# The global row normalised at the end, scored by halves, and more rounding on VectorE

## The chip, the cores and the metric

The kernel runs on one core of a Trainium2 chip. The metric is the device time of one execution in microseconds (us). A core has TensorE (PE) for matrix products, VectorE (DVE), ScalarE (ACT) and GpSimd (POOL) for elementwise work, and queues for DMA. Work in one engine is in program order; engines wait for each other by semaphores.

## What is computed

Two sequences of 1024 tokens (the model's batch of two) go through a two-layer transformer with banded attention, then a retention block and a mixture of experts. The change lies in the attention. Each of 12 heads (16 wide) attends to a window of 128-token blocks, and token 0 is "global": all see it, and it sees all 1024 keys, without a window. That second part is the "global row":

```
qg = q[:, :, g]                                     # g = token 0
sfull = jnp.einsum('bhgd,bhsd->bhgs', qg, k) + bias
og = jnp.einsum('bhgs,bhsd->bhgd', jax.nn.softmax(sfull, axis=-1), v)
out = out.at[:, :, g].set(og)
out = out.transpose(0, 2, 1, 3).reshape(b, s, d)
return out @ Wo.T + bo
```

For the windows, `softmax(scores)` is computed as exponentials in float32, which are split into a float16 value and a float16 rest, and both parts are multiplied with the values.

## The kernel before

The program makes four layer passes (2 sequences x 2 layers), and each runs the same code. In a pass there are a front (projections, transposes of q and k), U = 96 **units**, one for each block n of 128 queries and head h (u = 12n + h), and then the closing part (output projection y, norms, feed-forward). The last 12 units belong to block 7, whose window has two blocks (256 columns); the others have 384, or 256 for block 0.

The order is written by hand. Each engine's program calls its own `step(s)` for s from -24 to 113, and a unit passes through the engines with a fixed lag:

- **TensorE** at step s makes the scores of unit s into one of three banks (L1639 and L1642; it waits for the exponentials of unit s - 3) and then the value products of unit s - 4 (L1663; it waits for that unit's rounded parts). L1658 opens a group of six heads.
- **ScalarE** at step s takes the exponential of unit s twice: into p32 (float32, L806) and, for units that GpSimd serves, into p1 (float16, L808). A ring of six buffers (RING) holds them.
- **GpSimd** computes p2 = p32 - p1 for unit s - 1 (L609).
- **VectorE** serves each sixth unit (SHARE = 6: u % 6 == 5) in their place, at step u + 2: it casts p32 to p1 (L1127) and subtracts (L1128). It also combines each six heads (L1112, L1114, then L1152 at the end of the step).

From step ROW = 72 on, the global row goes through the same engines. TensorE multiplies the query of token 0 (q0s, one 12-column weight matrix for each head) with 1024 keys in two halves of 512: L1539, steps 72 to 83, one head a step, both halves, into banks 0 and 1. So both banks are complete only at step 83. VectorE takes the maxima (L1081 at step 84, L1131 and the minimum of the negated ones L1132 at step 85), ScalarE the exponentials with their sums (L772 at step 87, L775 at step 88), VectorE adds the sums, takes the reciprocal (L1084, L1085) and multiplies the 12 x 1024 row with it (L1086, step 89). TensorE transposes the row (L1546, step 91), ScalarE and VectorE make its float16 value (L779) and rest (L1090), and TensorE multiplies them with the values (L1554, steps 93 and 94, eight products each). VectorE selects each head's part (L1100, step 95, into og; rows 0 to 11 hold the value, 12 to 23 the rest). Last, six small products (L1567, L1569, step 100) sum the 24 rows of og with a column of ones.

Between them, at step 98, TensorE starts the output products y 0 and y 1 (L1413, L1414), which reuse banks 0 and 1 and therefore wait for L1100. After step 100 come the last transposes of att (L1622, L1623) and the sequence of y blocks, norms and feed-forward, in which VectorE adds and normalises what TensorE delivers.

## Time and profile before

| what | value |
|---|---|
| time, median of 3 runs | 891.1 us (891.08 to 892.95) |
| the profiled execution | 893.38 us, span of the core's work 891.6 us |
| TensorE products (PE) | 800.6 us, 90% of the span |
| TensorE weight loads (PEld) | 615.4 us, 69% |
| VectorE | 631.7 us, 71% |
| ScalarE | 561.2 us, 63% |
| GpSimd | 561.2 us, 63% |
| mean granted clock of TensorE | 0.964 of full |

The busy times are sums over the whole program; each stage has its own limit. The views used below are the timeline (start and duration of instructions on one engine, neighbours of one kind merged, and in brackets how long the engine was idle before and what ended that), and windows (busy time of each engine in a stretch, with the mean granted clock). The clock of TensorE has two levels, full (2.4 GHz) and half (1.2 GHz).

### The profile page before, as it was taken

Reading aid. Unit: us, or ns where it says so; the run is one execution under the profiler, and the core shown is the slowest. Engines: PE = TensorE matmul, PEld = TensorE weight load, DVE = VectorE, ACT = ScalarE, POOL = GpSimd, SP = SyncE. Lnnn points to the kernel's source line nnn. Section 1 sums busy time; section 2 is a strip of 40 time slices with the busy share of each in tenths; the row PEclk is TensorE's granted clock in tenths of the full one; section 3 lists DMA queues with packets and bytes.
Section 4 is the critical chain, followed back from the end, with each engine's and each line's share of the span. In section 5 each row is a group of like instructions: output and inputs, shape, how many; then the busy total and the mean of one; then the engine's idle time right before and its main releaser. Section 6 shows DMA issues by size and latency. Waiting matters only on the chain.

```text
span 891.6 us, 23616 instructions
## 1 busy us (share of the span) xinstructions
PE 800.6 (90%) x8467; PEld 615.4 (69%) x8467; DVE 631.7 (71%) x1903; ACT 561.2 (63%) x1558; POOL 561.2 (63%) x820
## 2 busy tenths in 40 slices
PE   6989999999999989989999889999998899786496
PEld 3767757667777666667777557777775568775495
DVE  4899956447999565568998462689993765987553
ACT  4878883348788843267888743678887444465264
POOL 5568876443488855464888663527886754767354
PEclk9999996999999979999999999999999999998699
DMA  3300020512000002330000006100000060501330
GB/s 81 104 8 4 3 52 4 167 40 80 3 4 3 22 26 98 109 94 26 4 3 3 22 1 203 52 33 4 3 4 2 1 202 1 214 2 60 93 106 25
DMA packets 38660, 43.84 MB, mean 49 GB/s; under 512 B 7227, under 2 KB 33946, under 8 KB 38410
## 3 DMA queue, kind: packets, MB, share of 16 engines
q1 hardware_dynamic: 18124, 19.30, 7.2%
q10 hardware_dynamic: 18148, 18.29, 6.6%
q0 software_dynamic: 2272, 4.74, 1.7%
q8 instruction: 69, 1.13, 0.5%
q14 instruction: 47, 0.38, 0.1%
HBM read 20.70 MB, written 21.59 MB: 47 GB/s over the span
## 4 chain that ended last, share of the span: by engine, by line
PE 64%; DVE 21%; POOL 5%; issue 4%; ACT 4%; DMA 2%; POOLq 0%; SPq 0%; DVEq 0%; ACTq 0%
PE bank L1419 7%; DVE p L1128 6%; PE bank L1590 5%; DVE nmx L1119 5%; PE bank L1663 5%; PE bank L1639 5%; PE bank L1714 4%; PE bank L1715 4%; PE bank L1528 4%; PE bank L1539 3%; PE bank L1593 3%; PE bank L1753 2%; PE bank L1642 2%; PE bank L1762 2%; DVE p L1127 2%
## 5 line engine op out<-in xcount | busy, mean ns | idle before, releaser
L609 POOL TENSOR_TENSOR p<-p 128x384 f16<-128x384 f32 (+1 forms) x320 | 286.0, 914 | 95.3 <-ACT p L808 91.4
L1119 DVE TENSOR_REDUCE nmx<-bank 128x1 f32<-128x384 f32 (+1 forms) x384 | 190.2, 510 | 14.0 <-PE bank L1593 9.4
L806 ACT ACTIVATE p<-bank 128x384 f32<-128x384 f32 (+1 forms) x384 | 170.2, 451 | 46.9 <-PE bank L1642 31.9
L1639 PE MATMUL bank<-stack 103*128 103x128 bf16 x1056 | 144.5, 221 | 5.3 <-ACT p L808 4.3
L808 ACT ACTIVATE p<-bank 128x384 f16<-128x384 f32 (+1 forms) x320 | 144.5, 452 | 0.0
L1642 PE MATMUL bank<-bandb,idb 128*128 128x128 bf16 x672 | 134.8, 221 | 0.0
L1590 PE MATMUL bank<-stack 100*128 100x384 bf16 (+1 forms) x384 | 120.3, 313 | 7.2 <-DVE nmx L1119 2.9
L1663 PE MATMUL bank<-vst,p 128*128 128x49 bf16 x2112 | 115.6, 185 | 9.5 <-DVE p L1128 9.1
L1663 PEld LDWEIGHTS bank<-vst,p 128*128 128x128 f16 x2112 | 89.4, 97 | 26.9 <-DVE p L1128 15.0
L1639 PEld LDWEIGHTS bank<-stack 103*128 103x128 bf16 x1056 | 87.8, 98 | 28.0 <-issue 15.6
L1593 PE MATMUL bank<-bandb,idb 128*128 128x128 bf16 x672 | 100.5, 219 | 0.0
L559 POOL TENSOR_TENSOR rstd<-ve,colc 128x1 f32<-128x1 f32 x64 | 35.1, 549 | 94.7 <-DVE ve L962 94.7
L1593 PEld LDWEIGHTS bank<-bandb,idb 128*128 128x128 bf16 x672 | 65.5, 97 | 20.5
L820 ACT ACTIVATE stack<-bank 96x1024 bf16<-96x1024 bf16 x64 | 65.1, 1017 | 19.3 <-PE bank L1528 17.8
L873 ACT ACTIVATE hid<-bank 128x512 f32<-128x512 f32 x48 | 28.7, 597 | 75.1 <-PE bank L1715 75.1
L1204 DVE TENSOR_TENSOR bank<-bank,resid 128x192 f32<-128x192 f32 x64 | 23.1, 360 | 71.4 <-PE bank L1419 71.4
L1528 PE MATMUL bank<-idb,hid 128*96 128x128 bf16 x768 | 59.1, 221 | 10.8 <-POOL hid L626 5.9
L1419 PE MATMUL bank<-w2s,hid 128*128 128x192 f32 x384 | 65.9, 328 | 3.0 <-ACT hid L873 1.7
L1528 PEld LDWEIGHTS bank<-idb,hid 128*96 128x96 bf16 x768 | 50.8, 123 | 24.2 <-issue 17.6
L1419 PEld LDWEIGHTS bank<-w2s,hid 128*128 128x128 f32 x384 | 62.2, 190 | 6.9 <-issue 5.1
L1642 PEld LDWEIGHTS bank<-bandb,idb 128*128 128x128 bf16 x672 | 65.3, 97 | 0.8
L1128 DVE TENSOR_TENSOR p<-p 128x384 f16<-128x384 f32 (+1 forms) x64 | 63.4, 991 | 2.2
(248 smaller groups left out, 1801.2 us busy)
## 6 DMA issues: line engine op xcount, KB each, us to landing
xs<-zrow ACTq DMA_DIRECT2D x8, 2193.0 KB, 12.6
xt<-xs SPq DMA_DIRECT2D x23, 129.0 KB
w2s<-in_w SPq DMA_DIRECT2D x4, 576.0 KB
mwbs<-in_mwb SPq DMA_DIRECT2D x1, 2064.0 KB, 8.7
mw2s<-in_mw SPq DMA_DIRECT2D x1, 2048.0 KB, 13.0
lnrow<-in_lnr SPq DMA_DIRECT2D x4, 480.0 KB
stack<-mtr SPq DMA_DIRECT2D x96, 3.0 KB
w1b<-in_w SPq DMA_DIRECT2D x4, 291.0 KB
```

The costliest lines, as they stand in the source:

```text
L609: nc.gpsimd.tensor_tensor(p2[:, u % RING, 0:w], p32[:, u % RING, 0:w], p1[:, u % RING, 0:w], ALU.subtract).then_inc(p2_pool, 1)
L806: ins = nc.scalar.activation(p32[:, s % RING, 0:w], ps[2 + s % 3][:, 0:w], ACT.Exp)
L808: ins = nc.scalar.activation(p1[:, s % RING, 0:w], ps[2 + s % 3][:, 0:w], ACT.Exp)
L1119: nc.vector.tensor_reduce(nmx[:, vn % 3, h:h + 1], nat_bank(v)[:, 0:w], AX.X, ALU.max, negate=True).then_inc(max_done, 1)
L1128: nc.vector.tensor_tensor(p2[:, u % RING, 0:w], p32[:, u % RING, 0:w], p1[:, u % RING, 0:w], ALU.subtract).then_inc(p2_dve, 1)
L1419: ins = mm(y, hid[:, m, blk(n % BPC)], w2s[:, m, :], start=m == 0, stop=m == FF // P - 1)
L1528: ins = nc.tensor.transpose(psb[3 + (3 * b + g) % 2][0:NPIECE, blk(h)], nat[:, b % 2, g * HG + h, :], idb[:, :])
L1590: mm(s_ps[:, 0:len(win) * P], q, stack[0:K_NAT, H + h, blk(win[0], len(win))], start=True, stop=False)
L1593: ins = mm(s_ps[:, blk(i)], idb[:, :], bandb[:, 0 if m < n else 1, :], start=False, stop=(i, m) == edges[-1])
L1639: ins = mm(ps[2 + s % 3][:, blk(i)], stack[0:K_ALL, H + h, blk(m)], stack[0:K_ALL, h, blk(n)], start=True, stop=m == n)
L1642: ins = mm(ps[2 + s % 3][:, blk(i)], idb[:, :], bandb[:, 1 if m < n else 0, :], start=False, stop=True)
L1663: ins = mm(out_ps, pt[:, w % RING, blk(a)], vst[:, m, h, :], start=False, stop=i == HH - 1 and a == len(win) - 1 and pt is p2)
```

## The change

Three things, in each of the four layer passes:

1. **Scores by halves.** The 24 products of the global row are made in another order: in steps 72 to 77 all twelve heads against the first half of the keys (bank 0), in steps 78 to 83 against the second half (bank 1), two a step as before. The semaphore f_mm counts twice. q0s holds each query twice (weights of 24 columns), so that the row's scores, maxima and exponentials stand in 24 rows, and the sum is there in all 24. VectorE writes q0s with two instructions.
2. **No scaling of the row.** L1086 is gone. The steps of the chain move: the maximum of bank 0 to step 80, that of bank 1 and the minimum to step 84, the exponentials from 87 and 88 to 85 and 86, the transposes from 91 to 89 (they wait for the exponentials alone), the float16 parts and the products with the values two steps up as well. The reciprocal is taken at step 92, and the six small products at step 100 use it in place of the ones.
3. **More units on VectorE.** Of the last twelve units, each third (86, 89, 92, 95) instead of each sixth (89, 95) is rounded by VectorE. ScalarE and GpSimd leave out their part of units 86 and 92.

```diff
+EXTRA = 3
+def on_dve(u):
+    return u % SHARE == SHARE - 1 or u >= U - 2 * SHARE and u % EXTRA == EXTRA - 1
...
@@ ScalarE
-                        if s == ROW + 15:
+                        if s == ROW + 13:
                             act.wait_ge(f_max, at(f_max, 1))
-                            nc.scalar.activation(pfull[:, 0, 0:CH], ps[0][0:H, :], ACT.Exp, bias=fst[:, 0:1],
+                            nc.scalar.activation(pfull[:, 0, 0:CH], ps[0][0:2 * H, :], ACT.Exp, bias=fst[:, 0:1],
                                                  accum_out=fst[:, 1:2]).then_inc(f_exp, 1)
...
-                            if s % SHARE != SHARE - 1:
+                            if not on_dve(s):
                                 ins = nc.scalar.activation(p1[:, s % RING, 0:w], ps[2 + s % 3][:, 0:w], ACT.Exp)
...
@@ VectorE
+                        for i in range(2):
+                            ins = nc.vector.tensor_scalar(
+                                q0s[0:K_NAT, :, :].rearrange("p a b -> p (a b)")[:, i * H:2 * H * H:2 * H + 1],
+                                stack[0:K_NAT, 0:H, 0], colc[0:K_NAT, 1:2], colc[0:K_NAT, 2:3], ALU.mult, ALU.add)
+                        ins.then_inc(glob_ready, 1)
...
+                        if s == ROW + 8:
+
+                            dve.wait_ge(f_mm, at(f_mm, 1))
+                            nc.vector.tensor_reduce(fst[:, 2:3], ps[0][0:2 * H, :], AX.X, ALU.max, negate=True)
                         if s == ROW + 12:
...
+                            dve.wait_ge(f_mm, at(f_mm, 2))
+                            ch.link(nc.vector.tensor_reduce(fst[:, 3:4], ps[1][0:2 * H, :], AX.X, ALU.max, negate=True))
+                            nc.vector.tensor_tensor(fst[:, 0:1], fst[:, 2:3], fst[:, 3:4], ALU.min).then_inc(f_max, 1)
...
+                        if s == ROW + 20:
+                            dve.wait_ge(f_exp, at(f_exp, 2))
+                            ch.link(nc.vector.tensor_tensor(fst[:, 3:4], fst[:, 1:2], fst[:, 2:3], ALU.add))
+                            nc.vector.reciprocal(fst[:, 0:1], fst[:, 3:4]).then_inc(f_norm, 1)
...
@@ TensorE
-                            for c in range(NC):
-                                ins = mm(ps[c][0:H, :], q0s[0:K_NAT, h, :], stack[0:K_NAT, H + h, c * CH:(c + 1) * CH],
-                                         start=h == 0, stop=h == H - 1)
-                            if h == H - 1:
+                            c, h = divmod(NC * h, H)
+                            for k in range(h, h + NC):
+                                ins = mm(ps[c][0:2 * H, :], q0s[0:K_NAT, k, :], stack[0:K_NAT, H + k, c * CH:(c + 1) * CH],
+                                         start=k == 0, stop=k == H - 1)
+                            if h + NC == H:
                                 ins.then_inc(f_mm, 1)
-                        if s == ROW + 19:
-                            pe.wait_ge(f_norm, at(f_norm, 1))
+                        if s == ROW + 17:
+                            pe.wait_ge(f_exp, at(f_exp, 2))
                             for n in range(NB):
-                                ins = nc.tensor.transpose(ps[0][:, n * H:(n + 1) * H], pfull[:, 1, blk(n)], idf[0:H, 0:H])
+                                ins = nc.tensor.transpose(ps[0][:, n * H:(n + 1) * H], pfull[0:H, 0, blk(n)], idf[0:H, 0:H])
...
+                            pe.wait_ge(f_norm, at(f_norm, 1))
                             for i in range(3):
-                                mm(ps[2][0:DLO, 0:1], og[:, i, 0:DLO], ones[0:2 * H, 0:1], start=i == 0, stop=i == 2)
+                                mm(ps[2][0:DLO, 0:1], og[:, i, 0:DLO], fst[:, 0:1], start=i == 0, stop=i == 2)
```

On VectorE of the first layer pass, from the maximum of the global row to the row's last use there, this stood in a row before (fst holds maxima and sums, p32, p1 and p2 the exponentials and their two parts, bank7 and den belong to a combine):

```order
L1081 TENSOR_REDUCE fst<-bank0 12x1
L1127 CAST p1<-p32 128x384
L1128 TENSOR_TENSOR p2<-p32,p1 128x384
L1131 TENSOR_REDUCE fst<-bank1 12x1
L1132 TENSOR_TENSOR fst<-fst 12x1
L1112 TENSOR_REDUCE bank7<-bank7 128x96
L1114 RECIPROCAL den<-bank7 128x6
L1152 TENSOR_TENSOR att<-bank7,den 128x96
L1084 TENSOR_TENSOR fst<-fst 12x1
L1085 RECIPROCAL fst<-fst 12x1
L1086 TENSOR_SCALAR hid<-hid,fst 12x1024
```

and this now, from the maximum of bank 1 on:

```order
L1097 TENSOR_REDUCE fst<-bank1 24x1
L1098 TENSOR_TENSOR fst<-fst 24x1
L1142 CAST p1<-p32 128x384
L1143 TENSOR_TENSOR p2<-p32,p1 128x384
L1127 TENSOR_REDUCE bank7<-bank7 128x96
L1129 RECIPROCAL den<-bank7 128x6
L1142 CAST p1<-p32 128x256
L1143 TENSOR_TENSOR p2<-p32,p1 128x256
L1164 TENSOR_TENSOR att<-bank7,den 128x96
L1101 TENSOR_TENSOR f12<-bank0,f12 128x8x12
```

The maximum of bank 0 and the multiplication of hid are no longer there, and a cast and subtraction of unit 86 stand inside the combine.

A little later on VectorE, before, from the float16 rest of the row (f12) to L1100's og:

```order
L1090 TENSOR_TENSOR f12<-bank0,f12 128x8x12
L1112 TENSOR_REDUCE bank6<-bank6 128x96
L1114 RECIPROCAL den<-bank6 128x6
L1152 TENSOR_TENSOR att<-bank6,den 128x96
L1100 TENSOR_TENSOR og<-bank1,own 24x3x96
L1100 TENSOR_TENSOR og<-bank0,own 24x3x96
```

and now:

```order
L1101 TENSOR_TENSOR f12<-bank0,f12 128x8x12
L1142 CAST p1<-p32 128x256
L1143 TENSOR_TENSOR p2<-p32,p1 128x256
L1105 TENSOR_TENSOR fst<-fst 24x1
L1106 RECIPROCAL fst<-fst 24x1
L1127 TENSOR_REDUCE bank6<-bank6 128x96
L1129 RECIPROCAL den<-bank6 128x6
L1142 CAST p1<-p32 128x256
L1143 TENSOR_TENSOR p2<-p32,p1 128x256
L1164 TENSOR_TENSOR att<-bank6,den 128x96
L1115 TENSOR_TENSOR og<-bank1,own 24x3x96
L1115 TENSOR_TENSOR og<-bank0,own 24x3x96
```

The sum and reciprocal of fst have come in between, and the cast and subtraction of unit 92 stand between the combine of bank 6 and og.

On ScalarE, before, from unit 86's exponentials to the float16 value of the row (f12):

```order
L806 ACTIVATE p32<-bank4 128x256
L808 ACTIVATE p1<-bank4 128x256
L772 ACTIVATE hid,fst<-bank0,fst 12x512
L806 ACTIVATE p32<-bank2 128x256
L808 ACTIVATE p1<-bank2 128x256
L775 ACTIVATE hid,fst<-bank1,fst 12x512
L806 ACTIVATE p32<-bank3 128x256
L808 ACTIVATE p1<-bank3 128x256
L806 ACTIVATE p32<-bank4 128x256
L806 ACTIVATE p32<-bank2 128x256
L808 ACTIVATE p1<-bank2 128x256
L779 ACTIVATE f12<-bank0 128x8x12
```

and now, from unit 84's:

```order
L817 ACTIVATE p32<-bank2 128x256
L819 ACTIVATE p1<-bank2 128x256
L783 ACTIVATE hid,fst<-bank0,fst 24x512
L817 ACTIVATE p32<-bank3 128x256
L819 ACTIVATE p1<-bank3 128x256
L786 ACTIVATE hid,fst<-bank1,fst 24x512
L817 ACTIVATE p32<-bank4 128x256
L817 ACTIVATE p32<-bank2 128x256
L819 ACTIVATE p1<-bank2 128x256
L817 ACTIVATE p32<-bank3 128x256
L819 ACTIVATE p1<-bank3 128x256
L790 ACTIVATE f12<-bank0 128x8x12
```

The two exponentials of the global row (hid) have moved from behind units 86 and 87 to behind units 84 and 85, unit 86 (the first of bank4) has no p1, and the float16 value comes before unit 89 instead of behind unit 90.

## Rows read from the trace of the kernel before

**Rows 1.** Timeline, TensorE, first layer's tail: start, duration, what [idle before <-releaser].

```profile
128.09 0.60 PE L1539 MATMUL bank<-stack,q0s 100*12 100x512 bf16 x2
...
133.15 0.23 PE L1639 MATMUL bank<-stack 103*128 103x128 bf16 x1 [1.07 <-ACT p L808]
...
134.95 1.03 PE L1546 MATMUL bank<-idf,hid 12*128 12x12 f32 x8 [1.36 <-DVE hid L1086]
...
137.46 2.13 PE L1554 MATMUL bank<-vst,f 128*24 128x294 bf16 x8
...
142.76 0.57 PE L1413 MATMUL bank<-woa,ata 96*128 96x192 f32 x2
```

**Rows 2.** Windows: stretch, length, busy of PE, PEld, DVE, ACT, POOL, clock, DMA.

```profile
132.10:134.95 2.85, 0.45 (x7) 0.34 (x7) 1.48 (x7) 2.85 (x11) 1.54 (x3) 0.87 0.60 165
134.20:141.00 6.80, 6.05 (x43) 4.39 (x44) 2.67 (x7) 3.37 (x13) 3.61 (x5) 0.50 0.02 4
687.10:690.60 3.50, 3.50 (x30) 2.72 (x29) 0.94 (x2) 1.57 (x5) 2.54 (x4) 0.51 0.00 0
```

**Rows 3.** Timeline, VectorE, first layer's tail.

```profile
128.73 0.68 DVE L1081 TENSOR_REDUCE fst<-bank 12x1 f32<-12x512 f32 x1 [1.08 <-PE bank L1539]
...
130.03 0.56 DVE L1128 TENSOR_TENSOR p<-p 128x384 f16<-128x384 f32 x1
...
131.22 0.55 DVE L1132 TENSOR_TENSOR fst<-fst 12x1 f32<-12x1 f32 x1
...
134.16 0.74 DVE L1086 TENSOR_SCALAR hid<-hid,fst 12x1024 f32<-12x1024 f32 x1
134.83 0.27 DVE L1127 CAST p<-p 128x256 f16<-128x256 f32 x1
135.13 0.78 DVE L1128 TENSOR_TENSOR p<-p 128x256 f16<-128x256 f32 x1
...
140.24 0.47 DVE L1112 TENSOR_REDUCE bank<-bank 128x96 f32<-128x288 f32 x1 [3.68 <-PE bank L1663]
...
141.76 0.81 DVE L1100 TENSOR_TENSOR og<-bank,own 24x288 f32<-24x288 f32 x2 [0.68 <-PE bank L1554]
143.06 0.53 DVE L1127 CAST p<-p 128x256 f16<-128x256 f32 x1 [0.49 <-ACT p L806]
```

**Rows 4.** Timeline, ScalarE, first layer's tail: the row's exponentials.

```profile
131.80 0.68 ACT L772 ACTIVATE hid<-bank,fst 12x512 f32<-12x512 f32 x1 [0.53 <-DVE fst L1132]
...
133.00 0.66 ACT L775 ACTIVATE hid<-bank,fst 12x512 f32<-12x512 f32 x1
```

**Rows 5.** Timeline, TensorE, tails of the second and the third layer pass.

```profile
311.69 0.60 PE L1539 MATMUL bank<-stack,q0s 100*12 100x512 bf16 x2
...
326.70 0.57 PE L1413 MATMUL bank<-woa,ata 96*128 96x192 f32 x2
...
498.49 0.60 PE L1539 MATMUL bank<-stack,q0s 100*12 100x512 bf16 x2
...
509.86 1.18 PE L1554 MATMUL bank<-vst,f 128*24 128x294 bf16 x8
...
512.07 0.57 PE L1413 MATMUL bank<-woa,ata 96*128 96x192 f32 x2
```

**Rows 6.** Timeline, GpSimd, first layer's tail, unit 94.

```profile
142.78 0.67 POOL L609 TENSOR_TENSOR p<-p 128x256 f16<-128x256 f32 x1 [1.31 <-ACT p L808]
```

**Rows 7.** Instructions on the tile q0s, VectorE: xcount, duration ns min/median/max.

```profile
L1065 DVE TENSOR_SCALAR q0s<-stack,colc x4: 303/304/305, 24.7 to 576.6; 100x12 bf16<-100x12 bf16 x4
```

**Rows 8.** Windows, 7 us around two other waits of TensorE.

```profile
383.25:390.25 7.00, 5.02 (x33) 3.64 (x32) 2.87 (x8) 3.47 (x6) 5.45 (x11) 0.76 0.33 86
567.10:574.10 7.00, 5.41 (x50) 4.20 (x51) 4.49 (x13) 4.91 (x10) 3.94 (x10) 1.00 0.35 93
```

**Rows 9.** Windows, 9 us from the y blocks on, first and third layer pass.

```profile
146.00:155.00 9.00, 8.51 (x35) 7.61 (x34) 8.23 (x31) 3.66 (x11) 7.48 (x14) 0.62 0.01 3
515.30:524.30 9.00, 7.08 (x37) 5.07 (x36) 8.24 (x31) 3.67 (x11) 7.45 (x14) 1.00 0.00 0
```

56 lines of the change are left out of this document (22 added, 34 removed).

## Prediction

> **What bounds the kernel now.** I read the page's busy shares first: TensorE 90%, no other engine above 71%. Then I looked for places where TensorE stands idle, and took the timeline of the end of a layer, engine by engine. Times below are those of the first layer pass; the other three repeat it, shifted.
>
> From unit 72 to unit 83 TensorE is packed: one step of scores, value products and two L1539 products every 1.07 us, no wait. The last L1539 starts at 128.09 [rows 1]. Then TensorE waits 1.07 us for ScalarE's exponentials and, 1.6 us later, 1.36 us for VectorE's L1086 [rows 1]. Of the 2.85 us before the L1546 transposes only 0.45 are busy [rows 2]. The clock follows: TensorE ran at full clock (2.4 GHz) until then, and then at half (1.2 GHz) for 6.8 us; the shortest such stretch of the four layers is 3.5 us [rows 2]. So the L1554 products stand in a slow stretch. What releases the transposes is one chain through the global row: L1539 ends, maximum of bank 0 (L1081, 128.73), behind it unit 83's rounding, maximum of bank 1, minimum until 131.77 (L1132) [rows 3]; ScalarE's two exponentials of the row, at 131.80 and 133.00, with unit 87's pair between them [rows 4]; the sum, the reciprocal, and L1086 from 134.16 to 134.90 [rows 3]. The output products y 0 and y 1 start at 142.76 [rows 1]. I measure a tail from the last L1539 to that L1413: 14.67 us here, 15.01 in the second layer, 13.58 in the third [rows 5]; the fourth repeats the third within 0.05.
>
> **Scores by halves, maximum earlier.** The number of L1539 products stays; bank 0 is finished six steps sooner, its maximum (0.68 us) moves into VectorE's idle time before 128.73, at no cost: were that cover gone it would cost its 0.68. Bank 1's maximum starts where bank 0's did: 128.73 + 0.68 + 0.55 for the minimum + 0.05 of hand-over gives 130.0 instead of 131.77. Queued behind it on VectorE is unit 83's rounding, which ran from 129.64 and now starts at 130.0, so unit 83's value products come about 0.4 us later. The weights become 24 columns wide instead of 12; no row of before shows such a load, but loads lie beside products that last 0.60 us in pairs [rows 1], and I price it at nothing.
>
> **Exponentials at steps 85 and 86.** ScalarE then never waits for the maximum (0.53 us before). From L772 at 131.80 to L775 at 133.00 is 1.20 us with one pair between [rows 4]. From 130.05 the same 1.20 puts the second half at 131.25 and its sum at 132.0. Queued behind: unit 85's pair ends at 131.35, which holds unit 88's scores for 0.15 us. The transposes, moved up by two steps and waiting only for the exponentials, start at 132.05 instead of 134.95.
>
> **The multiplication goes.** L1086 (0.74 us [rows 3]) and the wait for it disappear; what is late next is the copy of the transposed row: it now stands on ScalarE behind the second half (131.25, 0.66 us), one activation of unit 86 (0.26, half of the 0.52 that a pair takes in the 1.20) and the pairs of units 87 and 88, so it starts at 133.2 and ends near 133.45. VectorE's subtraction ends near 133.85. In between TensorE does units 89 and 90 and waits 0.5 us in two pieces. The 16 L1554 products start at 133.9 instead of 137.46. At full clock eight of them last 1.18 us (509.86) against 2.13 at half clock [rows 1, 5]. The third layer's stretch from 509.86 to 512.07, at full clock, holds eight of them, two steps, L1658 and four units' remaining products in 2.2 us; at that pace the sixteen, five steps, L1658 and the two transposes of att take 4.2, and TensorE stands behind unit 95's scores and unit 91's products at 138.1.
>
> **Units 86 and 92 on VectorE.** ScalarE is rid of two activations, GpSimd of two subtractions; neither is what TensorE waits for there. VectorE gets two pairs. A cast took 0.27 to 0.53 us, a subtraction of this width 0.78; the nearest lower bound is 0.56, of a wider one at 130.03 in an idle stretch of GpSimd [rows 3]. Unit 86 lands in a gap of VectorE and ends with the copy above: nothing. Unit 92 does cost. It stands after the combine L1112, which waits for unit 89's products (now 137.4), and ahead of L1100. So: combine until 138.0, unit 92 until 139.05 to 139.3, the rest of the combine 0.25, L1100 0.81 [rows 3], and y 0 starts at 140.3 at the earliest. TensorE stands idle from 138.1 but for 0.25 us of units 92 and 93. Without this unit L1100 would be ready near 139.1: about 1.1 us of the gain is given away. I take y 0 at 140.5, a tail of 12.4 us; with the lower bound of the subtraction 12.0, with 0.5 more 12.9.
>
> Here the rows show engines in each other's way: the cast at 143.06 took 0.53 us, with a subtraction of GpSimd on from 142.78 [rows 3, 6], and the one at 134.83 took 0.27. The Trainium skill (SBUF — State Buffer, section "Who interferes with whom") says that the two engines take one port pair in turn and that the later one is blocked until the earlier has finished. By that rule unit 92's cast would wait for the whole 0.67 us of GpSimd's unit 93 and every tail would be 12.9 us, 2.0 us worse in the sum, 888.9; by the row, 0.26 us of delay, it is 12.4. The trace of 143.06 agrees, since that subtraction had 0.39 us left.
>
> **One instruction more at a layer's front**: q0s is written twice. The instruction lasts 0.30 us [rows 7]; between nothing and 0.30 a layer. I take 0.3 us in all, since TensorE has other work queued there.
>
> **The sum.** Tails: 14.67 - 12.4 = 2.3, then 2.6, 1.2 and 1.2: 7.3 us. Less 0.3 at the fronts: 7.0. All of it reaches the end, because the y blocks behind start in the same order and later loads were finished long before.
>
> **What the clock does decides the rest.** The idle time between 138.1 and 140.5 is 2.1 us with 0.25 busy in it, and right behind stand the one-column products L1567. Before, 2.4 us with 0.45 busy brought the clock down in all four layers [rows 2]; elsewhere some 2.0 us of standing idle were followed by a fall (mean clock 0.76) and 1.6 us were not (1.00) [rows 8]. The new 2.1 us come in two pieces and are near to both cases. So I expect a fall, but not in each layer: in two of the four. A stretch of 3.5 us at half clock costs half of it, 1.75, where TensorE is on the path; here y 2 has some 0.4 to spare before VectorE wants it, so 1.4. Two falls: 2.8. Forecast: 7.0 - 2.8 = 4.2 us. The profiled execution took 893.4 us with a span of 891.6, 2.3 above the median of 891.1; the falls need not be the same in number in each execution. I take the 4.2 from the median: 886.9.
>
> **Rivals.**
> - The clock never falls in the tails: what speaks for it is that 1.6 us of standing idle passed without a fall [rows 8], and that the new stretch is cut by two units' products. Then the 7.0 stay, and the first layer's y stretch can win too: it ran at a mean clock of 0.62 where the third's ran at 1.00, with TensorE busy for 8.5 of nine us against 7.1 [rows 9]; of these 1.4 I count 1.2. 891.1 - 8.2 = 882.9. Chance 0.22.
> - The clock falls in all four: 7.0 - 5.6 = 1.4, so 889.7. For it: 2.1 us are as long as the 2.0 us after which it fell [rows 8], and the layers are alike. Chance 0.18.
> - Slower. Unit 92, kept out by GpSimd's units 93 and 94, delays L1100 to near 141 (tail 12.9 to 13.2); the long idle brings the clock down in each layer (1.4), and it stays down through the y stretch of one layer more than before, for 1.2, the first layer's price. Then the four tails, 56.8, less 4 x 13.05 are 4.6 gained; 5.6, 1.2 and 0.3 are lost: 2.5 slower, 893.6. With three more y stretches slow it would be 4.9 slower. It decides from the point at which y 0 starts after about 140.8. Chance 0.10.
> - Nothing arrives: the tail is set by the exponentials, scores and GpSimd's subtractions alone, whatever the row does. Against it: TensorE's second wait names L1086 and no exponential. The order of instructions shows the move made. 891.1. Chance 0.05.
>
> **Numbers.** Forecast 0.45 (884.5 to 889.2), the others as given. Measurement can tell 0.2%, 1.8 us, from no change: faster is below 889.3, slower above 892.9. Faster: 0.45 + 0.22 + 0.05 of the all-fall case = 0.72; same 0.18; slower 0.10. The range for 8 in 10 holds the forecast, the no-fall case and most of the all-fall case: 882.0 to 890.5, the low end for tails of 12.0 where no clock falls.
>
> **What would show it.** Right: in each tail the waits of 1.07 and 1.36 are gone, the transposes (L1546's successor) start 3.8 to 4.1 us after the last row product, the L1554 products run at full clock and 3.5 us earlier, and a new idle stretch of 1.5 to 2.5 us stands before y 0, released by VectorE's subtraction of unit 92 and by L1100 under its new number. Wrong: the slow stretch stays around the L1554 products; the transposes wait for ScalarE past 133; y 0 starts later than 13 us after the last row product without a slow clock; or the fronts of the layers grow by more than 0.3 us.

## The result, and the profile after

| | before | after |
|---|---|---|
| time, median of 19 runs each | 893.07 us (889.39 to 898.84) | 887.14 us (883.03 to 891.76) |
| ratio, with its 95% interval | | 0.9936 (0.9918 to 0.9954) |
| the profiled execution | 893.38 us, span 891.6 | 884.74 us, span 883.0 |
| TensorE products | 800.6 us | 792.0 us |
| mean granted clock of TensorE | 0.964 | 0.976 |

The kernel became faster by 5.9 us; 4.2 were forecast. The time lies 0.2 us from the forecast of 886.9, but the forecast was taken from a median of 891.1 (3 executions), and over 19 that of the kernel before is 893.07. So the closeness is in part luck, and it says little about the reasons, as the experiments show. The two profiled executions differ by 8.6 us, more than the medians, and of the 19 executions of the changed kernel the profiled one has the highest mean granted clock: 0.976, with a median of 0.969 and a lowest of 0.964. So the breakdown below is of a pair in favour of the changed kernel, and how many slow stretches its usual execution has is not shown.

A **tail** is the stretch from the start of the last pair of row products to the start of y 0, as in the prediction. A **slow stretch** is one in which TensorE's granted clock is half. A **y block** is one of the output products with the norm behind it.

The line numbers moved. On TensorE: L1539 is now L1552 (row products), L1546 is L1559 (transposes), L1554 is L1567 (products with the values), L1639 is L1653 (scores), L1663 is L1677 (value products), L1413 is L1425 (y 0). On VectorE: L1097 and L1098 are the second maximum and the minimum, L1142 and L1143 cast and subtraction, L1164 the end of a combine, L1115 writes og. On ScalarE L783 and L786 are the row's exponentials. L620 is GpSimd's subtraction.

The first layer's tail on TensorE, to be held against [rows 1]:

```profile
128.63 0.60 PE L1552 MATMUL bank<-stack,q0s 100*24 100x512 bf16 x2
...
131.91 0.23 PE L1653 MATMUL bank<-stack 103*128 103x128 bf16 x1 [0.39 <-ACT p L819]
...
132.62 0.66 PE L1559 MATMUL bank<-idf,hid 12*128 12x12 f32 x8
...
133.40 0.26 PE L1677 MATMUL bank<-vst,p 128*128 128x49 bf16 x4
...
133.68 0.37 PE L1677 MATMUL bank<-vst,p 128*128 128x49 bf16 x4
134.31 2.13 PE L1567 MATMUL bank<-vst,f 128*24 128x294 bf16 x8 [0.27 <-DVE f L1101]
...
136.97 1.22 PE L1567 MATMUL bank<-vst,f 128*24 128x294 bf16 x8
...
140.78 0.37 PE L1677 MATMUL bank<-vst,p 128*128 128x49 bf16 x8 [0.79 <-DVE p L1143]
141.71 0.56 PE L1425 MATMUL bank<-woa,ata 96*128 96x192 f32 x2 [0.56 <-issue]
```

Counted from the last row product, the transposes start at 3.99 us (6.86 before), the products with the values at 5.68 (9.37 before), y 0 at 13.08 (14.67 before). But TensorE still waits: 0.39 and 0.27 us early, 0.79 for VectorE's subtraction of unit 92, and 0.56 before y 0. The first eight L1567 last 2.13 us as L1554 did, at half clock. The slow stretch has begun before the 0.27 us, at 133.67 (mean clock 0.83 from 133 to 134 us): the four L1677 at 133.68 already last 0.37 us where those at 133.40 last 0.26. In the third layer, to be held against [rows 5], the same places are these:

```profile
492.40 0.60 PE L1552 MATMUL bank<-stack,q0s 100*24 100x512 bf16 x2
...
498.08 1.18 PE L1567 MATMUL bank<-vst,f 128*24 128x294 bf16 x8 [0.37 <-DVE f L1101]
...
504.28 0.56 PE L1425 MATMUL bank<-woa,ata 96*128 96x192 f32 x2 [0.56 <-issue]
```

Here the eight products last 1.18 us and y 0 starts at 11.88. The windows say why (stretch, length, busy time and count of PE, PEld, DVE, ACT and POOL, mean granted clock, DMA). After:

```profile
128.63:141.71 13.08, 10.97 (x144) 7.65 (x142) 7.71 (x22) 8.35 (x30) 7.29 (x11) 0.87 0.29 74
134.00:137.00 3.00, 2.73 (x18) 1.54 (x17) 1.96 (x5) 0.85 (x4) 1.39 (x3) 0.50 0.15 42
315.00:318.00 3.00, 2.78 (x16) 1.62 (x17) 1.87 (x5) 0.85 (x4) 1.30 (x3) 0.50 0.01 3
492.40:504.28 11.88, 9.68 (x144) 7.05 (x142) 7.71 (x22) 8.35 (x30) 7.30 (x11) 1.00 0.01 2
383.00:392.00 9.00, 8.79 (x83) 6.52 (x82) 7.42 (x22) 7.58 (x15) 5.86 (x13) 1.00 0.38 113
146.00:155.00 9.00, 7.09 (x33) 4.44 (x32) 8.10 (x31) 3.52 (x9) 8.16 (x16) 1.00 0.01 2
```

Before, the same kind of stretch, from the last row product to y 0, in the first and the third layer:

```profile
128.09:142.76 14.67, 12.08 (x145) 8.48 (x142) 7.36 (x19) 9.21 (x32) 8.23 (x11) 0.77 0.26 67
498.49:512.07 13.58, 10.99 (x144) 7.67 (x142) 7.36 (x19) 9.20 (x32) 8.22 (x11) 0.87 0.01 2
```

Before, TensorE was idle for 2.59 us of each tail (14.67 - 12.08, and 13.58 - 10.99). After, it is idle for 2.11 in the first (13.08 - 10.97) and for 2.20 in the third (11.88 - 9.68). The idle time fell by 0.4 to 0.5 us, while the tails fell by 1.59, 1.86, 1.70 and 1.66 us, 6.81 in sum. What fell is for the most part the time that the products take: before, every tail has a stretch at half clock, of 6.8 us in two layers and 3.4 in two; after, the first two tails have one of 3.4 us and the last two have none.

The rest of the 8.6 us: the y blocks of the first layer run at full clock now (the 146 to 155 window, 0.62 in [rows 9]), the third layer's do not (the next fence), 0.83 less in sum over the four, from y 0 to the first feed-forward product; a slow stretch between the second and the third pass is gone (383 to 392, clock 1.00; 0.76 in [rows 8]), 1.9 us.

```profile
505.70:512.50 6.80, 6.80 (x36) 6.43 (x35) 5.33 (x20) 1.25 (x6) 3.36 (x6) 0.50 0.01 2
```

So the third pass is not without a fall: it came 1.4 us behind y 0, after the waits of 0.79 and 0.56, lasted 6.8 us, and took 11.72 us where the other passes take 10.94 from y 0 to the first feed-forward product. In the fourth pass one of 3.4 us stands there, at 690.0, and costs nothing (10.93).

The first layer's last row product stands 0.54 us later than before. The added instruction on q0s is not the reason: behind it VectorE goes on at 25.17 us against 25.15, as far apart as the two kernels were ahead of it, and from there to the 55th microsecond they stay 0.02 to 0.03 us apart. Then 0.43 us of it arise at one cast of VectorE, of the first unit that it rounds (before, then after):

```profile
55.94 0.27 DVE L1127 CAST p<-p 128x256 f16<-128x256 f32 x1
```

```profile
55.97 0.70 DVE L1142 CAST p<-p 128x256 f16<-128x256 f32 x1
```

In both kernels a subtraction of GpSimd had started 0.12 us earlier. Before, that one took 0.93 us and the cast 0.27; after, it took 0.67 and the cast 0.70, and TensorE waited 0.66 us instead of 0.23 for this unit. The instructions of the two kernels are the same here, and in ten of the twelve other kernels of this study the cast takes 0.27, in e11 and e12 0.69. So this is an accident of the execution, not an effect of the change.

### The profile page after: what moved, and what is told of

It is laid out like the page before. It is cut to its first block, busy times and chain, and to the rows that moved or that the text cites. A ratio compares the mean times of both kernels' runs of the same rounds, so it can differ in the third digit from the quotient of the medians.

```text
span 883.0 us, 23620 instructions
## 1 busy us (share of the span) xinstructions
PE 792.0 (90%) x8467; PEld 610.7 (69%) x8467; DVE 634.1 (72%) x1919; ACT 556.7 (63%) x1550; POOL 553.2 (63%) x812
## 4 chain that ended last, share of the span: by engine, by line
PE 61%; DVE 21%; issue 6%; POOL 5%; ACT 4%; DMA 2%; POOLq 0%; SPq 0%; ACTq 0%; DVEq 0%
PE bank L1431 7%; DVE p L1143 6%; PE bank L1604 5%; DVE nmx L1134 5%; PE bank L1653 4%; PE bank L1677 4%; PE bank L1728 4%; PE bank L1729 4%; PE bank L1540 4%; PE bank L1552 3%; PE bank L1607 3%; PE bank L1656 2%; PE bank L1767 2%; PE bank L1776 2%; DVE p L1142 2%
## 5 line engine op out<-in xcount | busy, mean ns | idle before, releaser
L620 POOL TENSOR_TENSOR p<-p 128x384 f16<-128x384 f32 (+1 forms) x312 | 278.1, 911 | 92.2 <-ACT p L819 83.7
L1653 PE MATMUL bank<-stack 103*128 103x128 bf16 x1056 | 142.5, 219 | 2.5 <-ACT p L819 1.6
L819 ACT ACTIVATE p<-bank 128x384 f16<-128x384 f32 (+1 forms) x312 | 141.2, 452 | 0.0
L1677 PE MATMUL bank<-vst,p 128*128 128x49 bf16 x2112 | 115.3, 185 | 12.8 <-DVE p L1143 12.5
L1677 PEld LDWEIGHTS bank<-vst,p 128*128 128x128 f16 x2112 | 88.8, 96 | 29.8 <-DVE p L1143 18.8
L1653 PEld LDWEIGHTS bank<-stack 103*128 103x128 bf16 x1056 | 87.2, 97 | 23.7 <-issue 14.6
L1143 DVE TENSOR_TENSOR p<-p 128x384 f16<-128x384 f32 (+1 forms) x72 | 67.8, 942 | 2.5
L1540 PE MATMUL bank<-idb,hid 128*96 128x128 bf16 x768 | 58.7, 219 | 10.8 <-POOL hid L637 5.9
```

Source lines behind the costliest of these rows:

```text
L620: nc.gpsimd.tensor_tensor(p2[:, u % RING, 0:w], p32[:, u % RING, 0:w], p1[:, u % RING, 0:w], ALU.subtract).then_inc(p2_pool, 1)
L819: ins = nc.scalar.activation(p1[:, s % RING, 0:w], ps[2 + s % 3][:, 0:w], ACT.Exp)
L1143: nc.vector.tensor_tensor(p2[:, u % RING, 0:w], p32[:, u % RING, 0:w], p1[:, u % RING, 0:w], ALU.subtract).then_inc(p2_dve, 1)
L1540: ins = nc.tensor.transpose(psb[3 + (3 * b + g) % 2][0:NPIECE, blk(h)], nat[:, b % 2, g * HG + h, :], idb[:, :])
L1653: ins = mm(ps[2 + s % 3][:, blk(i)], stack[0:K_ALL, H + h, blk(m)], stack[0:K_ALL, h, blk(n)], start=True, stop=m == n)
L1677: ins = mm(out_ps, pt[:, w % RING, blk(a)], vst[:, m, h, :], start=False, stop=i == HH - 1 and a == len(win) - 1 and pt is p2)
```

## The experiments

Two theories stood against each other. By the **chain theory** the gain is what the prediction summed: the row's chain is shorter, so y 0 comes earlier. By the **clock theory** the chain's length hardly matters; what was lost before was products at half clock behind a long idle stretch, and an edit that breaks up that stretch gives the same gain with the chain as it was. The tails of all kernels that ran, from the last row product to y 0 in each of the four layer passes of the profiled execution:

| kernel | tails, us | sum | ratio to before (95%) |
|---|---|---|---|
| before | 14.67 15.01 13.58 13.54 | 56.80 | 1 |
| the changed kernel | 13.08 13.15 11.88 11.88 | 49.99 | 0.9936 (0.9918 to 0.9954) |
| e1, row only | 12.94 12.93 12.94 12.94 | 51.75 | 0.9929 (0.9907 to 0.9951) |
| e2, rounding only | 14.67 14.08 14.92 14.04 | 57.71 | 1.0010 (0.9994 to 1.0026) |
| e3, row scaled | 14.31 15.28 14.57 14.62 | 58.78 | 1.0057 (1.0035 to 1.0080) |
| e4, head by head | 11.89 11.96 13.07 13.08 | 50.00 | 0.9915 (0.9894 to 0.9936) |
| e5, og first | 11.17 12.41 11.17 11.17 | 45.92 | 0.9915 (0.9889 to 0.9940) |
| e7, waits filled | 11.85 11.92 11.85 11.85 | 47.47 | 0.9926 (0.9908 to 0.9944) |
| e8, before, filled | 12.07 12.06 12.07 12.06 | 48.26 | 0.9925 (0.9907 to 0.9943) |
| e9, unit 91, og first | 12.66 12.67 11.14 12.67 | 49.14 | 0.9920 (0.9895 to 0.9946) |
| e10, og first, filled | 11.29 11.36 11.29 11.29 | 45.23 | 0.9864 (0.9845 to 0.9882) |
| e11, y filled too | 11.27 11.34 11.27 11.27 | 45.15 | 0.9868 (0.9849 to 0.9886) |
| e12, row only, filled | 12.38 12.39 12.39 12.39 | 49.55 | 0.9913 (0.9900 to 0.9926) |
| e13, row scaled, filled | 13.24 13.31 13.24 13.24 | 53.03 | 0.9955 (0.9937 to 0.9972) |

Kernels e1 to e4 shared a chip and a set of runs of the kernel before, so did e5 to e9, and so did e10 to e13. Medians of before were 891.48, 888.98 and 892.49 us in the three. Ratios are comparable across them only within their intervals. The tails are those of one profiled execution of each kernel.

### e1: the row's part alone

The changed kernel with units 86 and 92 left to ScalarE and GpSimd.

```diff
-EXTRA = 3
+EXTRA = 6
```

> The changed kernel, but units 86 and 92 are rounded by GpSimd and ScalarE as before (EXTRA = 6). My theory (the gain is the row's chain; unit 92 on VectorE gives about 1 us a layer back): the stretch from the last row product to y 0 shrinks from 11.9 us (a layer pass of the changed kernel without a slow clock in it) to 10.8 to 11.1, and the time is 3 to 4 us below the changed kernel's: ratio to before 0.989 to 0.991. Rival (the relief of ScalarE and GpSimd carries part of the gain): ScalarE's two further activations push the row's float16 copy back by 0.26 us or more, the stretch stays at 11.9 or grows, ratio 0.993 to 0.997.

885.68 us, a ratio of 0.9929 against 0.9936 with the rounding on VectorE: the rounding adds nothing to the time that can be measured. The 10.8 to 11.1 us expected did not come, since no tail ran at full clock. TensorE, first layer's tail:

```profile
134.99 1.65 PE L1567 MATMUL bank<-vst,f 128*24 128x294 bf16 x8 [0.46 <-DVE f L1101]
...
141.22 0.27 PE L1677 MATMUL bank<-vst,p 128*128 128x49 bf16 x4 [0.23 <-POOL p L620]
141.85 0.27 PE L1677 MATMUL bank<-vst,p 128*128 128x49 bf16 x4 [0.35 <-POOL p L620]
```

The waits of 0.79 and 0.56 us at the tail's end have become 0.23 and 0.35, for GpSimd. In exchange the wait before L1567 grew from 0.27 to 0.46 and every one of the four tails has a slow stretch. Against a tail of the changed kernel with a slow stretch (13.08, 13.15) these are only 0.14 to 0.21 us shorter. The window of the first:

```profile
129.03:141.97 12.94, 11.41 (x145) 7.70 (x142) 6.07 (x17) 8.75 (x32) 7.50 (x12) 0.87 0.28 74
```

TensorE is idle for 1.53 us (12.94 - 11.41), against 2.11 to 2.20 in the changed kernel. So the two units on VectorE do cost it some 0.6 us of waiting a tail, and here most of that is taken back by the slow stretch, which falls on more products. An estimate for e1's tail at full clock is that idle time plus the 9.68 us that the products take in the changed kernel's third tail: 11.2 us.

### e2: the rounding alone

The kernel before, with its row as it was, and units 86 and 92 on VectorE.

```diff
+EXTRA = 3
+def on_dve(u):
+    return u % SHARE == SHARE - 1 or u >= U - 2 * SHARE and u % EXTRA == EXTRA - 1
...
-                            if s % SHARE != SHARE - 1:
+                            if not on_dve(s):
...
-                        if 0 <= u < U and u % SHARE == SHARE - 1:
+                        if 0 <= u < U and on_dve(u):
```

> The kernel before with the third part of the change alone: VectorE rounds units 86, 89, 92, 95. My theory: nothing waits for ScalarE or GpSimd there, unit 92 stands ahead of the selection of og, so each tail grows by 0.5 to 1.1 us (third layer pass 13.6 to 14.1 or more) and the ratio to before is 1.002 to 1.005. Rival (this part brings the gain): tails shorter, ratio 0.994 to 0.998.

892.02 us, no difference, and not the 1.002 to 1.005 expected. The waits of 1.07 and 1.35 us stand as they were. So the third part of the change does nothing to the time that can be measured, alone or on top of the rest.

### e3: the multiplication put back

The changed kernel, but the row is scaled before its transposes, as before; everything else keeps its new place.

```diff
+                        if s == ROW + 15:
+                            dve.wait_ge(f_exp, at(f_exp, 2))
+                            ch.link(nc.vector.tensor_tensor(fst[:, 3:4], fst[:, 1:2], fst[:, 2:3], ALU.add))
+                            ch.link(nc.vector.reciprocal(fst[:, 3:4], fst[:, 3:4]))
+                            nc.vector.tensor_scalar(pfull[:, 1, :], pfull[:, 0, :], fst[:, 3:4], None,
+                                                    ALU.mult).then_inc(f_norm, 1)
...
-                            pe.wait_ge(f_exp, at(f_exp, 2))
+                            pe.wait_ge(f_norm, at(f_norm, 1))
```

> The changed kernel with the row scaled before the transposes again (sum, reciprocal, multiplication at step 87; the small products use the column of ones). My theory: the transposes start at 5.0 to 5.2 us after the last row product instead of 4.0, the L1567 products 0.7 to 1.0 us later, tails 0.7 to 1.0 us longer, time 3 to 4 us above the changed kernel's: ratio to before 0.996 to 0.998. Rival (the copy behind ScalarE's exponentials hides the multiplication): the L1567 products start within 0.3 us of where they did, ratio 0.993 to 0.995.

895.96 us: slower than the kernel before, and outside what either side expected. TensorE, first layer's tail:

```profile
131.81 0.23 PE L1654 MATMUL bank<-stack 103*128 103x128 bf16 x1 [0.39 <-ACT p L819]
...
133.62 0.67 PE L1561 MATMUL bank<-idf,hid 12*128 12x12 f32 x8 [1.03 <-DVE hid L1103]
...
135.11 0.35 PE L1678 MATMUL bank<-vst,p 128*128 128x49 bf16 x4 [0.27 <-DVE p L1145]
```

A wait of 1.03 us stands before the transposes, which at their early place have units 89 to 95 queued behind them. Moving the chain's steps up was therefore no gain by itself here; it pays only because the multiplication is gone. (e3 also has units 86 and 92 on VectorE; by e2 these alone do not change the time.) Against the changed kernel the tails are 8.8 us longer in sum.

### e4: the scores head by head

The changed kernel, with both halves of a head scored together again and both maxima at one step.

```diff
-                            c, h = divmod(NC * h, H)
-                            for k in range(h, h + NC):
+                            for c in range(NC):
...
-                        if s == ROW + 8:
+                        if s == ROW + 12:
```

> The changed kernel with the row's scores in the old order (one head a step, both halves), so that both maxima are taken after the last product. My theory: 0.68 us more on the chain ahead of the exponentials, hidden in part since ScalarE is 0.3 us behind anyway: transposes 0.4 to 0.7 us later, tails 0.3 to 0.7 longer, ratio to before 0.994 to 0.997. Rival (earlier maximum is idle ahead of ScalarE): no change against the changed kernel, 0.993 to 0.994.

884.41 us, a ratio of 0.9915 and so no longer than with the halves (the 0.994 to 0.997 expected is out), and tails of 11.89 to 13.08. The first maximum's 0.68 us do not reach y 0. They come out as a wait elsewhere, for unit 83's rounding, before its value products:

```profile
132.33 0.33 PE L1676 MATMUL bank<-vst,p 128*128 128x49 bf16 x6 [0.82 <-DVE p L1143]
```

In the changed kernel 0.39 us for ScalarE stand there instead. The halves bring nothing that can be measured.

### e5: og before unit 92

The changed kernel, with L1115 one step earlier in VectorE's order: og no longer stands behind unit 92 and its combine.

```diff
-                        if s == U - 1:
+                        if s == U - 2:
```

> The changed kernel with VectorE's selection of og moved up by one step, ahead of the combine and of unit 92's rounding. My theory (TensorE's last wait before y 0, 0.56 us, is for og, which stands behind unit 92 on VectorE): that wait goes, the 0.8 us wait for unit 92 stays; last row product to y 0 11.2 to 11.4 us without a slow clock (changed kernel: 11.9), about 2 us off the time, ratio to before 0.990 to 0.993. Rival (the stretch is set elsewhere, as by the output products' other waits): 11.8 to 11.9 stays, ratio 0.993 to 0.994.

880.08 us. TensorE, first layer's tail; the 0.56 us before y 0 are gone and y 0 follows unit 92's products at once:

```profile
139.75 0.37 PE L1677 MATMUL bank<-vst,p 128*128 128x49 bf16 x8 [0.79 <-DVE p L1143]
139.96 0.57 PE L1425 MATMUL bank<-woa,ata 96*128 96x192 f32 x2
```

At full clock the tail is 11.17 us instead of 11.88, so og's place behind unit 92 cost 0.71. Unit 92 was paid for by what was queued behind it. The times alone do not tell this kernel from the changed one (0.9915 and 0.9936, with intervals that overlap); the tails at full clock do. The second tail, with a slow stretch, is 12.41: one such stretch costs 1.24 us here.

### e7: the changed kernel, its waits filled

The waits themselves are left where they are, and one is added, for the copies of the transposed att, ahead of the fill for unit 92; in front of each TensorE multiplies something that nobody reads, 64 columns a product. So the clock is put to the test without the chain.

```diff
+                    def fill(k):
+                        for _ in range(k):
+                            mm(ps[5][:, 448:512], idb[:, :], bandb[:, 0, 0:64], start=True, stop=True)
...
+                                fill(10)
...
+                            fill(20)
...
+                            if s == U - 8:
+                                fill(13)
...
+                            if w == U - 4:
+                                pe.wait_ge(at_copied, at(at_copied, NB - 1))
+                                fill(28)
```

fill(13) stands before unit 88's scores, fill(10) before the wait for f12's rest, fill(28) before unit 92's value products, fill(20) before the wait for og.

> The changed kernel with products whose result nobody reads (64 columns, into unused columns of bank 5) in the four places of the tail where TensorE waits: 13, 10, 28 and 20 of them, some 0.03 us each. They take no data dependent time from the engines around. If the slow clock in the tails is due to these waits, no tail has a slow stretch, all four are 11.9 to 12.2 us, and the time is 2 to 4 us below the changed kernel's: ratio to before 0.989 to 0.992. Rival (the fall has to do with the whole stretch, or the fill only delays): a slow stretch stays in two tails or more, ratio 0.993 or above.

881.69 us, a ratio of 0.9926 where 0.989 to 0.992 was expected, and no tail with a slow stretch. The second tail is 11.92 and not 11.85: unit 92's subtraction takes 0.07 us longer there, as it does in the changed kernel. First layer's tail (the L1546 here are the fillers):

```profile
132.04 0.54 PE L1546 MATMUL bank<-bandb,idb 128*128 128x64 bf16 x13
...
134.99 1.18 PE L1572 MATMUL bank<-vst,f 128*24 128x294 bf16 x8
...
141.16 0.58 PE L1425 MATMUL bank<-woa,ata 96*128 96x192 f32 x2
```

y 0 starts 11.85 us after the last row product, as in the undisturbed third layer of the changed kernel (11.88). Filling does not shift the chain; it shows its length at full clock.

### e8: the kernel before, its two waits filled

Nothing of the change, only fillers in the two waits of [rows 1].

```diff
+                            fill(48)
...
+                            if s == U - 6:
+                                fill(38)
```

> The kernel before with such products in its two long waits: 38 ahead of unit 90's scores, 48 ahead of the row's transposes. This gives the price of the clock alone, with the chain through the row as long as before. My theory: no slow clock in the tails, all four 12.2 to 12.8 us instead of 13.5 to 15.0, transposes still 6.9 us after the last row product, 4 to 6 us off the time: ratio to before 0.993 to 0.996. Rival (the slow clock costs little, since others are late anyway): tails above 13.2, ratio 0.998 to 1.000.

881.89 us, a ratio of 0.9925: the kernel before gains as much by useless products as it did by the change. TensorE, first layer's tail (L1534 are the fillers, L1559 the products with the values):

```profile
132.24 1.27 PE L1534 MATMUL bank<-bandb,idb 128*128 128x64 bf16 x38
...
133.75 1.56 PE L1534 MATMUL bank<-bandb,idb 128*128 128x64 bf16 x48
135.27 0.66 PE L1551 MATMUL bank<-idf,hid 12*128 12x12 f32 x8
...
136.76 1.18 PE L1559 MATMUL bank<-vst,f 128*24 128x294 bf16 x8
...
140.47 0.57 PE L1413 MATMUL bank<-woa,ata 96*128 96x192 f32 x2
```

The transposes start 6.87 us after the last row product, as late as in the kernel before (6.86). The chain is as long as it was, and yet y 0 comes at 12.07 instead of 14.67. And in the same set of runs e7 took 881.69 us: with the clock held in their tails, the kernel before and the changed one take the same time. Windows of this kernel, a tail and then a stretch of y blocks:

```profile
128.40:140.47 12.07, 11.90 (x231) 9.38 (x228) 7.36 (x19) 9.11 (x32) 8.21 (x11) 1.00 0.35 84
325.00:333.00 8.00, 7.51 (x28) 6.41 (x27) 7.20 (x27) 3.20 (x8) 7.26 (x14) 0.57 0.00 1
```

The tails run at full clock; the fall has moved into the y blocks behind them in three of four passes, where it costs less: from y 0 to the first feed-forward product 12.07 us instead of 11.09. That gives back some 3 of the 8.5 us that the tails gained; in the first pass, where the kernel before took 12.09, it is 11.09 here, which leaves 1.9 given back.

### e9: unit 91 instead of unit 92

As e5, with VectorE serving unit 91, which comes one step sooner.

```diff
-    return u % SHARE == SHARE - 1 or u >= U - 2 * SHARE and u % EXTRA == EXTRA - 1
+    return u % SHARE == SHARE - 1 or u in (U - 10, U - 5)
```

> The changed kernel with og selected one step earlier and with unit 91 instead of 92 on VectorE, where VectorE is idle for 3 us. My theory: GpSimd, rid of unit 91, has unit 92 ready 0.5 us earlier; then unit 93 is the last to come; last row product to y 0 11.0 to 11.2 us without a slow clock, 0.7 to 0.9 below the changed kernel, ratio to before 0.988 to 0.992. Rival (units 92 and 93 queue on GpSimd behind each other as in the kernel with EXTRA = 6): 11.6 to 11.8, ratio 0.992 to 0.994.

880.23 us against 880.08 for e5: the same. The wait of 0.79 us is gone, 0.23 and 0.35 for GpSimd's subtractions have come (as in e1), and at full clock the tail is 11.14 against 11.17. But three of the four tails have a slow stretch, of 1.5 us each, against one in e5, and the time does not show the 3.2 us by which its tails are longer. Behind the tails the account is the other way round: e5 has slow stretches from 558 to 562 us and from 757 to 760, and e9 ran both at full clock. A fall saved in one place turned up in another.

### e10: both remedies together

e5's order and e7's fillers, but for those before y 0, where there is no wait left.

```diff
-                        if s == U - 1:
+                        if s == U - 2:
...
-                            fill(20)
```

> The kernel with og selected one step earlier (e5) and the fill of e7 in the three waits that are left. If TensorE's own work plus its waits make the stretch from the last row product to y 0 (9.6 to 9.8 us of work in every version at full clock) and the clock adds the rest, all four tails are 11.1 to 11.3 us without a slow clock; ratio to before 0.986 to 0.990. Rival (y stretches and the rest of the program fall into the slow clock instead, as in the filled kernel before): tails as said, but ratio 0.991 or above.

879.65 us, 0.9864 (0.9845 to 0.9882): 12.8 us below the kernel before in the same set of runs; no other version of this study has a lower ratio. Its first tail on TensorE:

```profile
139.46 0.99 PE L1546 MATMUL bank<-bandb,idb 128*128 128x64 bf16 x28
...
140.49 0.57 PE L1425 MATMUL bank<-woa,ata 96*128 96x192 f32 x2
```

y 0 at 11.29 and not at e5's 11.17: the 28 products last 0.99 us where the wait was 0.79.

### e11: the y blocks filled too

```diff
+                            if i < 4:
+                                for _ in range(12):
+                                    mm(ps[7][:, 0:64], idb[:, :], bandb[:, 0, 0:64], start=True, stop=True)
```

These stand before the first four transposes of z in the y blocks, in waits of 0.32 to 0.50 us.

> The same with 12 such products, into bank 7, ahead of each of the first four transposes of the norm stretch behind y 0, where TensorE waits 0.3 to 0.5 us for VectorE. A norm stretch at full clock took 10.9 us from y 0 to the first feed-forward product, a slow one up to 12.1. If that is the clock's price, none is above 11.1 here and the time is 0.5 to 2 us below e10's; rival (the fill stands in the way, since the waits are short): stretches of 11.1 to 11.6 us, time as e10's or above.

880.08 us, no different from e10. From y 0 to the first feed-forward product it takes 10.95 us in each pass, in both kernels. e10 had one slow stretch there, from 145.8 to 149.2 us, which cost nothing: VectorE has the pace of this stage (busy for 3.72 of the four us from 146 to 150).

### e12: the row alone, filled

e7 without units 86 and 92 on VectorE.

```diff
-EXTRA = 3
+EXTRA = 6
```

> e7 (the changed kernel with the waits filled) with units 86 and 92 on GpSimd: the part on VectorE without the clock's chance. In the unfilled kernels the stretch was 11.9 us with it at full clock and 12.9 without it with one slow stretch in it. The prediction said that the part gives 1.1 us a layer away: then tails of 10.8 here. The rival, which the trace of the unfilled kernel speaks for (GpSimd's units 92 and 93 were waited for 0.23 and 0.35 us): 11.6 to 11.8, ratio within 0.001 of e7's 0.9926.

884.20 us, tails of 12.39, longer than e7's 11.85 and outside what either side expected. This run does not tell what it was made for. The fillers at the tail's end were sized for waits of 0.79 and 0.56 us. Here the waits to be covered were 0.23 and 0.35 (e1), while the 48 products keep TensorE for 1.4 us whatever comes, behind one more wait of 0.36:

```profile
139.54 0.99 PE L1546 MATMUL bank<-bandb,idb 128*128 128x64 bf16 x28 [0.36 <-ACT atb L826]
...
140.57 0.74 PE L1546 MATMUL bank<-bandb,idb 128*128 128x64 bf16 x20
...
141.15 0.57 PE L1425 MATMUL bank<-woa,ata 96*128 96x192 f32 x2
```

So the worth of units 86 and 92 on VectorE at a held clock was not measured; the estimate from e1's idle time is a loss of some 0.7 us a tail (11.88 - 11.2). At the clock as it falls it is nothing that the times show, by e1 and e2.

### e13: the scaled row, filled

e3 with e7's fillers and 36 more products in the wait of 1.03 us.

```diff
+                            fill(36)
...
+                                fill(10)
...
+                            fill(20)
```

> e3 (the changed kernel, but the row scaled before the transposes) with its waits filled. The multiplication's price without the clock: if a tail is TensorE's work plus its waits, the waits of 0.4, 1.0, 0.3, 0.8 and 0.6 us make 12.7 to 13.1 us in all four layers, 0.9 to 1.2 above e7; ratio to before 0.996 to 0.998. Rival (what e3 lost was the clock): tails of 12.0 to 12.3, ratio 0.992 to 0.994.

887.24 us. No tail is slow, and three are 13.24 us and one 13.31: 1.39 more than e7's 11.85, and above the 12.7 to 13.1 expected. That is the price of the multiplication and the wait for it on the moved-up chain, free of the clock; 5.6 us in four layers. It is an upper bound: fill(10) stands where e3 had no wait, f12's rest is done at 135.62 us and its products start at 135.84, so up to 0.2 us a tail are the filler's. The times show less of it: 3.0 us between e12 and e13, which shared their set of runs, with tails 3.5 us apart in sum, and 0.0029 or 2.6 us by the ratios of e7 and e13, whose tails are 5.6 apart. Of the 8.8 us by which e3's tails exceed the changed kernel's, the other 3.2 would be clock. And 13.24 is more than the 12.07 of e8, by 1.2 us a tail at full clock. Not all of it is the price of the early places: e13 also has unit 92 on VectorE ahead of og, which cost 0.71 in e5, and a version without it was not run.

## Why the prediction was right, and where its reasons were not

**What bounds the kernel** was read rightly in one point that counted: the two waits, 2.43 us together, bring the clock down, and the products behind them pay. e8 shows it directly: cover the waits, leave the chain, and 14.67, 15.01, 13.58 and 13.54 become 12.07.

**The early chain** came as worked out. Exponentials of the row 1.95 us after the last row product (1.96 forecast), transposes at 3.99 (3.96), products with the values at 5.68 (5.81). On ScalarE and VectorE, against [rows 3, 4]:

```profile
129.27 0.68 DVE L1097 TENSOR_REDUCE fst<-bank 24x1 f32<-24x512 f32 x1 [1.09 <-PE bank L1552]
129.99 0.16 DVE L1098 TENSOR_TENSOR fst<-fst 24x1 f32<-24x1 f32 x1
```

```profile
130.58 0.66 ACT L783 ACTIVATE hid<-bank,fst 24x512 f32<-24x512 f32 x1
...
131.76 0.66 ACT L786 ACTIVATE hid<-bank,fst 24x512 f32<-24x512 f32 x1
```

The minimum took 0.16 us and not L1132's 0.55. ScalarE gave the 0.4 back: it had the pair of unit 84 on until then. Unit 88's scores were held for 0.39 us, against 0.15 forecast.

**"Tails: 14.67 - 12.4 = 2.3, then 2.6, 1.2 and 1.2"** is the step that failed, though its total nearly came true. It takes a tail of before with its slow clock and subtracts one without, and books the difference to the chain. The chain's own part is what both kernels do at the same clock: 12.07 (e8) against 11.88 (third layer) or 11.85 (e7), 0.2 us a layer and 0.8 in four. The other 6.0 of the 6.8 us are clock, in this pair of executions. In the median the share is not known, but e7 and e8, 881.69 and 881.89 us in one set of runs, say the same of the times. By the prediction's own 12.4 the chain would even have become 0.3 us longer. That 12.4 was too large as well: 11.88 was measured, 2.1 us in four layers, and this is most of the difference between the 4.5 us of tails that the forecast left after two falls (7.3 - 2.8) and the 6.8 of the profile. That a wrong account gave a time 0.2 us off is luck. What the shorter chain did bring is smaller pieces of waiting: 0.39, 0.3, 0.79 and 0.56 in four places instead of 1.07 and 1.36 in two near each other. In two of four tails that kept the clock; in the other two, and behind y 0 in the third pass, it did not.

**Unit 92 on VectorE** was priced at about 1.1 us of the gain. The mechanism, a unit in front of og in VectorE's order, is right, and the term was too large: 0.71 for og's place behind it by e5, and some 0.7 for the whole part by the estimate from e1. The new idle stretch before y 0 was forecast at 2.1 us with 0.25 of it busy; there are 0.79 + 0.56 = 1.35 us of waits. VectorE, first layer:

```profile
139.61 0.25 DVE L1142 CAST p<-p 128x256 f16<-128x256 f32 x1
139.90 0.82 DVE L1143 TENSOR_TENSOR p<-p 128x256 f16<-128x256 f32 x1
140.64 0.25 DVE L1164 TENSOR_TENSOR att<-bank,den 128x96 f32<-128x96 f32 x1
140.81 0.80 DVE L1115 TENSOR_TENSOR og<-bank,own 24x288 f32<-24x288 f32 x2
...
142.08 0.43 DVE L1143 TENSOR_TENSOR p<-p 128x256 f16<-128x256 f32 x1
```

```profile
139.77 0.67 POOL L620 TENSOR_TENSOR p<-p 128x256 f16<-128x256 f32 x1 [1.45 <-PE bank L1677]
```

The cast of 0.25 us was not held back, in this pass or in the other three: it had started before GpSimd. The subtraction behind it, on while GpSimd was, took 0.82 us; one of the same shape at 142.08, with GpSimd idle, took 0.43. The Trainium skill (SBUF — State Buffer, section "Who interferes with whom") says that the shared port pair is an exclusive lock. The trace agrees in kind, 0.39 us for an overlap of 0.54, and the price that the prediction worked out by that rule, the whole 0.67 on the cast and tails of 12.9, did not come, because the cast was first. Where GpSimd's subtraction had started 0.12 us first, at the 56th microsecond, the cast took 0.70 in the changed kernel and 0.27 in the kernel before.

**The clock's part.** Two slow tails of four were forecast, and two there were in the one execution that was profiled. But the place was another: the fall was expected in the idle time before y 0, and it came at 133.67, just ahead of the L1567 products and five to seven microseconds sooner, when TensorE had waited only 0.39 us in this tail. That is one of the prediction's own signs of being wrong ("the slow stretch stays around the L1554 products"), met in two layers. Where the fall was expected, behind the waits before y 0, it came in the third pass alone, and cost 0.78 us there (11.72 against 10.94). The price of a slow tail was 1.20 and 1.27 us and not 1.4 (13.08 and 13.15 against 11.88; 1.24 in e5). Of the rival without a fall one piece also came true: the first layer's y blocks run at full clock. Nothing was forecast on the slow stretch between the second and the third pass, and it gave 1.9 us.

**Scores by halves** were to start the second maximum early at no cost, and did, and brought nothing (e4). **No scaling** is what carries the change: up to 1.39 us a tail at full clock in the new order, and e3 without it is slower than before. **The fronts** cost nothing that can be read, not 0.3 in all: from the first feed-forward product of a pass to the first row product of the next it takes 144.00 us in both kernels in the second pass. The weights of 24 columns were priced at nothing; the twelve steps of row products take 12.89 us in each pass and took 12.83, 0.2 in all.

**The rival "slower"** rested on tails of 12.9 to 13.2 from unit 92 and slow clocks in all of them. Its first term was wrong (0.39 us more on unit 92's subtraction, 0.71 for the unit), so its point of decision, y 0 after 140.8, was passed in two layers only by the clock.

## What to carry to other kernels

When the profile shows the clock at half behind a wait, split what the wait costs into idle time and slow products before you price a remedy. Some products whose result nobody reads, put into the wait, are a cheap experiment that gives the second part alone, and at times they are the remedy: here they gained as much (0.9925) as a restructured chain (0.9936), and the two together, with one line of order mended, twice that (0.9864). Size them to the wait, no longer: 0.99 us of them in a wait of 0.79 pushed y 0 back by 0.12, and in e12 they hid what was to be measured.

A step on an in-order engine is as dear as what is queued behind it. Moving steps up without making their input early turned a gain into a loss (e3), and one line moved in front of a unit gave 0.7 us a layer (e5).

## What the runs showed of the hardware that was not expected

- The clock falls behind much shorter waits than those of before, and the same code falls in some passes and not in others. In two tails of the changed kernel it fell 1.8 us behind a wait of 0.39 us, the only one that the timeline names since the last row product; in the other two tails the same 0.39 and then 0.37 were not followed by a fall.
- A fall avoided at one place may come at another. With all tails of e8 at full clock, the y blocks of three passes ran at a mean clock of 0.57 for eight microseconds; between e5 and e9 the slow stretches changed places in the same way. So a ratio of two kernels on one profiled tail says little about their times.
- The minimum of one column took 0.55 us before (L1132) and 0.16 after (L1098). GpSimd had a subtraction on beside both, and both minima ended within 0.01 us of its end (131.77 and 131.76, 130.14 and 130.14). That fits a VectorE that is held until GpSimd is done; no run here tests it.
- Which of the two is held can turn between executions of the same instructions: with GpSimd's subtraction started 0.12 us ahead in both, VectorE's cast took 0.27 us beside a subtraction of 0.93 once, and 0.70 beside one of 0.67 the other time. What decides it is open.
